# Half of the last stage's preparation moved into the scans before it, and the experts' units reordered and written out

## The reference, cut to what matters

```python
logits = xf @ gate_w
topk_vals, topk_idx = jax.lax.top_k(logits, 2)
gates = jax.nn.softmax(topk_vals, axis=-1)
h = jnp.einsum('nc,ech->neh', xf, w1) + b1[None]
h = jax.nn.gelu(h, approximate=False)
eo = jnp.einsum('neh,ehc->nec', h, w2) + b2[None]
comb = jnp.einsum('nk,nke->ne', gates, onehot)
out = jnp.einsum('ne,nec->nc', comb, eo)
```

## Time and profile before

| what | value |
|---|---|
| median of three runs | 977.3 us |
| the profiled execution, its own time | 978.52 us |
| its span | 976.7 us |
| busy in the span | TensorE 82%, VectorE 84%, ScalarE 68%, GpSimd 25% |
| first and last scan begin | 558.6 and 745.8 us |
| first expert product begins | 775.8 us |

### The profile page before, as it was taken

How to read it: one execution, slowest core, us unless ns; L and a number is a source line. 1 busy time by engine, 2 the same in 40 slices (tenths; PEclk the granted TensorE clock), 3 DMA queues, 4 the chain that set the end, 5 groups by cost and what they waited for, 6 DMA issues and landing times.

```text
span 976.7 us, 13030 instructions
## 1 busy us (share of the span) xinstructions
PE 801.6 (82%) x4241; PEld 414.7 (42%) x4241; DVE 818.1 (84%) x764; ACT 668.0 (68%) x1233; POOL 239.6 (25%) x132
## 2 busy tenths in 40 slices
PE   4579989999999999986375475677665679999998
PEld 2312212221222222223353355555554548888886
DVE  6788858887888888895888889999999846888886
ACT  2305757776777777775133597999994368888885
POOL 3800000000000000010100057888987501221220
PEclk9857979999999999999778688999999579999999
DMA  8422321212022110001200234455552021221221
GB/s 187 114 65 61 82 76 34 61 34 64 31 70 79 47 53 12 12 12 39 64 0 6 86 110 154 152 198 190 202 205 90 0 90 61 69 66 64 65 65 43
DMA packets 41524, 76.05 MB, mean 78 GB/s; under 512 B 7560, under 2 KB 25456, under 8 KB 40432
## 3 DMA queue, kind: packets, MB, share of 16 engines
q1 hardware_dynamic: 41464, 75.30, 24.7%
HBM read 64.99 MB, written 8.85 MB: 76 GB/s over the span
## 4 chain that ended last, share of the span: by engine, by line
PE 54%; ACT 17%; DVE 17%; issue 5%; SPq 4%; DMA 1%; POOL 0%; ACTq 0%; DVEq 0%; POOLq 0%
PE ps L1441 12%; PE ps L1462 11%; ACT dtb L912 8%; PE ps L1412 6%; PE ps L1696 6%; PE ps L1697 6%; PE ps L1698 6%; ACT abar L886 5%; DVE nmax L1066 3%; DVE hst L1201 2%; PE ps L1513 1%; SPq L521 1%; SPq L531 1%; DVE fx L454 1%; DVE fx L455 1%
## 5 line engine op out<-in xcount | busy, mean ns | idle before, releaser
L789 ACT ACTIVATE prob<-ps 128x512 f32<-128x512 f32 x512 | 265.0, 605 | 114.5 <-PE ps L1441 112.1
L1069 DVE TENSOR_REDUCE nmax_k<-ps 128x2 f32<-128x1024 f32 x224 | 262.4, 1219 | 45.5 <-PE ps L1412 44.3
L1441 PE MATMUL ps<-qs,ks 96*128 96x512 bf16 x512 | 165.8, 396 | 8.3 <-ACT prob L789 3.8
L717 POOL TENSOR_TENSOR hc<-hst,cbr 128x1024 f32<-128x1024 f32 x64 | 154.6, 2438 | 35.3 <-DVE hst L1201 23.7
L1201 DVE TENSOR_TENSOR_SCAN hst<-abar,ps 128x1024 f32<-128x1024 f32 x64 | 142.8, 2273 | 4.0 <-ACT abar L886 2.1
L1462 PE MATMUL ps<-prob,vq 128*16 128x512 f32 x1024 | 135.9, 608 | 0.8 <-ACT prob L789 0.7
L1284 DVE TENSOR_TENSOR act_l<-act_t,act_h 128x1024 fp32r<-128x1024 f32 x64 | 91.0, 1431 | 37.2 <-ACT act_h L996 37.2
L1441 PEld LDWEIGHTS ps<-qs,ks 96*128 96x128 bf16 x512 | 40.1, 98 | 169.5 <-ACT prob L789 109.0
L992 ACT ACTIVATE act_t<-ps,b_now 128x512 f32<-128x512 f32 x128 | 82.9, 683 | 25.4 <-PE ps L1698 25.4
L912 ACT ACTIVATE dtb<-dtxt,bt 128x128 f32<-128x128 f32 x328 | 99.8, 389 | 0.0
L1611 PE MATMUL ps<-ident,dtb 128*128 128x128 f32 x328 | 50.4, 291 | 51.2 <-DVE hst L1201 41.6
(11 more groups left out here) (192 smaller groups left out, 1146.6 us busy)
## 6 DMA issues: line engine op xcount, KB each, us to landing
cbr<-s_dram SPq DMA_DIRECT2D x64, 512.0 KB, 4.2
gate<-c_dram SPq DMA_DIRECT2D x8, 1024.0 KB, 7.5
qs<-q_dram SPq DMA_DIRECT2D x16, 288.0 KB
ks<-k_dram SPq DMA_DIRECT2D x48, 96.0 KB
o_dram<-o_sb SPq DMA_DIRECT2D x16, 256.0 KB, 2.0
wf<-in_L_ffn_w SPq DMA_DIRECT2D x8, 256.0 KB, 2.8
wfq<-in_L_ffn_w SPq DMA_DIRECT2D x8, 256.0 KB, 3.1
km<-k_dram SPq DMA_DIRECT2D x56, 32.0 KB
```

The costliest lines, as they stand in the source:

```text
L717: nc.gpsimd.tensor_tensor(hc[:, slot], hst[:, slot], cbr[:, slot], ALU.mult).then_inc(s_hc, 1)
L789: nc.scalar.activation(prob[:, n % 8], ps[:, 4 + (first + n) % 3], ACT.Exp, scale=ATT_SCALE).then_inc(s_exp, 1)
L1069: nc.vector.tensor_reduce(nmax_k[:, half, kk, 2 * pair:2 * pair + 2, qt], ps[:, 2 * pair:2 * pair + 2, :], AX.X, ALU.max, negate=True).the ...
L1441: nc.tensor.matmul(ps[:, 4 + (first + n) % 3], ks[p][:, kt // 4, j, kt % 4 * P:(kt % 4 + 1) * P], qs[p][:, half, j, :], start=True, stop=T ...
```

## The change

For batch 0, the norm, the turning and rounding, the logits, the choice of experts, the gates and the split of expert 0's weights now stand among the scans of batch 1, at written positions m. The ranking by 8 x 8 comparisons becomes two rounds of maximum, comparison and removal (`pick_two`). For batch 1, the same steps stand among the first units, which take experts 0 and 1 on batch 0's chunks first. The first product of unit 0 waits for the last scan, and the last two totals come behind it. b2 is added in the instruction that multiplies by the gate, and the matmuls and copies for it are gone, as are the copies of b1 (L1273). The remainder of x is taken from PSUM. Dynamic loops over scans and units are written out. Buffers of the last stage are laid over those of the scans with spacers (`over`), so that what is written early lies on nothing in use. The core of the diff:

```diff
-UNITS = 2 * CHUNKS
+UNITS = EXPERTS * CHUNKS
+FIRST_UNITS = ((0, 0), (0, 1), (1, 0), (1, 1), (0, 2), (0, 3), (1, 2), (1, 3))
+FAR_BELOW = -3.0e38
...
+        def unit_of(m):
+
+            return FIRST_UNITS[m] if m < len(FIRST_UNITS) else divmod(m, CHUNKS)
+
+        def last_unit(e):
+
+            return max(m for m in range(UNITS) if unit_of(m)[0] == e)
...
+            def first_gates(b):
+                w = slice(b * SEQ, (b + 1) * SEQ)
+                sp.wait_ge(s_combt, b + 1)
+                sp.dma_start(c_dram[:, w], comb_t[:, w]).then_inc(s_comb_out, 16)
+                sp.wait_ge(s_comb_out, 16 * (b + 1))
+                for e in range(2):
+                    sp.dma_start(gate[:, e, w], c_dram[e:e + 1, w].to_broadcast([P, SEQ])).then_inc(s_gate[e], 16)
+
+            def next_expert(e):
+                sp.wait_ge(s_w_l, e - 1)
+                load_expert(e, e % 2)
+
+            first_gates(0)
+            next_expert(2)
+            next_expert(3)
+            first_gates(1)
+            for e in range(2, EXPERTS):
+                sp.wait_ge(s_moe, 2 + last_unit(e - 2) + 1)
+                load_gate(e, e % 2)
+                if e + 2 < EXPERTS:
+                    next_expert(e + 2)
...
+            def upper_weights(e):
+
+                p = e % 2
+                pool.wait_ge(s_w12[p], 32 * (e // 2 + 1))
+                if e >= 2:
+                    pool.wait_ge(s_l2, 2 + last_unit(e - 2) + 1)
                 nc.gpsimd.tensor_tensor(w12_h[:, p], w12[p], zero[:].unsqueeze(2).to_broadcast([P, 2, HIDDEN]),
                                         ALU.subtract).then_inc(s_w_h, 1)
+
+            def lower_weights(e):
+
+                p = e % 2
                 pool.wait_ge(s_w_h, e + 1)
                 nc.gpsimd.tensor_tensor(w12_l[:, p], w12[p], w12_h[:, p].bitcast(F32), ALU.subtract).then_inc(s_w_l, 1)
 
...
+            pool.wait_ge(s_normed, 6)
+            for m in range(BATCH * NSTATE):
+                outflow(m)
+                if m == 14:
+                    upper_weights(0)
+                if m == 22:
+                    lower_weights(0)
+                if m == 41:
+                    norm_pool(3, 0)
+            upper_weights(1)
+            lower_weights(1)
             norm_pool(3, 1)
+            for e in range(2, EXPERTS):
+                upper_weights(e)
+                lower_weights(e)
...
+            def second_gate(b):
+                act.wait_ge(s_diff, b + 1)
+                nc.scalar.activation(top[:, 3, 8 * b:8 * b + 8], top[:, 2, 8 * b:8 * b + 8], ACT.Exp).then_inc(s_ediff, 1)
+
+            def turned_gates(b):
+                act.wait_ge(s_combt_ps, b + 1)
+                nc.scalar.activation(comb_t[:, b * SEQ:(b + 1) * SEQ].rearrange("e (g t) -> e g t", t=BANK), ps[0:EXPERTS, 4:6],
+                                     ACT.Copy).then_inc(s_combt, 1)
...
+                if m == 41:
+                    norm_act(3, 0)
+                if m == 51:
+                    turn_and_round(0)
+                    turn_and_round(1)
+                if m == 59:
+                    second_gate(0)
+            turned_gates(0)
...
+            for m in range(UNITS):
+                unit(m)
+                if m == 1:
+                    norm_act(3, 1)
+                if m == 2:
+                    turn_and_round(2)
+                    turn_and_round(3)
+                if m == 4:
+                    second_gate(1)
+                if m == 5:
+                    turned_gates(1)
...
+            def lower_x(c):
+                w = slice(c * BANK, (c + 1) * BANK)
+                dve.wait_ge(s_xh, c + 1)
+                nc.vector.tensor_tensor(xl[:, w], ps[:, 4 + c % 2], xh[:, w].bitcast(F32), ALU.subtract).then_inc(s_xl, 1)
+
+            def pick_two(b):
+
+                t = slice(8 * b, 8 * b + 8)
+                row = lambda n: bc(top[:, n, t], EXPERTS)
+                order = first[:].unsqueeze(1).to_broadcast([P, 8, EXPERTS])
+                dve.wait_ge(s_lgps, b + 1)
+                dve_step(nc.vector.tensor_copy(lg[:, t], ps[:, 4, 0:8 * EXPERTS].rearrange("p (t e) -> p t e", e=EXPERTS)))
+                left = lg[:, t]
+                for n in range(2):
+                    dve_step(nc.vector.tensor_reduce(top[:, n, t], left, AX.X, ALU.max))
+                    dve_step(nc.vector.tensor_tensor(key[:, n, t], left, row(n), ALU.is_equal))
+                    dve_step(nc.vector.tensor_tensor(key[:, n, t], key[:, n, t], order, ALU.mult))
+                    dve_step(nc.vector.tensor_reduce(top[:, 6 + n, t], key[:, n, t], AX.X, ALU.max))
+                    dve_step(nc.vector.tensor_tensor(is01[:, n, t], key[:, n, t], row(6 + n), ALU.is_equal))
+                    if n == 0:
+                        dve_step(nc.vector.scalar_tensor_tensor(comb[:, t], is01[:, 0, t], FAR_BELOW, lg[:, t], ALU.mult, ALU.add))
+                        left = comb[:, t]
+                nc.vector.tensor_tensor(top[:, 2, t], top[:, 1, t], top[:, 0, t], ALU.subtract).then_inc(s_diff, 1)
+
+            def gates(b):
+
+                t = slice(8 * b, 8 * b + 8)
+                dve.wait_ge(s_ediff, b + 1)
+                dve_step(nc.vector.tensor_scalar(top[:, 4, t], top[:, 3, t], 1.0, None, ALU.add))
+                dve_step(nc.vector.reciprocal(top[:, 4, t], top[:, 4, t]))
+                dve_step(nc.vector.tensor_tensor(top[:, 5, t], top[:, 3, t], top[:, 4, t], ALU.mult))
+                for n in range(2):
+                    ins = nc.vector.tensor_tensor(is01[:, n, t], is01[:, n, t], bc(top[:, 4 + n, t], EXPERTS), ALU.mult)
+                dve_step(ins)
+                nc.vector.tensor_tensor(comb[:, t], is01[:, 0, t], is01[:, 1, t], ALU.add).then_inc(s_comb, 1)
...
+                if m == 20:
+                    dve_step(nc.vector.tensor_reduce(first[:], tri[:], AX.X, ALU.add))
+                    dve_step(nc.vector.tensor_scalar(first[:], first[:], -1.0, float(EXPERTS), ALU.mult, ALU.add))
                 if m == NSTATE + 2:
                     add_scanned(0)
...
+                if m == 36:
+                    norm_dve_a(3, 0)
+                if m == 40:
+                    norm_dve_var(3, 0)
+                if m == 44:
+                    norm_dve_scale(3, 0)
+                if m == 49:
+                    lower_x(0)
+                    lower_x(1)
+                if m == 53:
+                    pick_two(0)
+                if m == 56:
+                    gates(0)
...
+            def combine(m):
+
+                e, c = unit_of(m)
                 w = slice(c * BANK, (c + 1) * BANK)
-                if c == 0:
-                    dve.wait_ge(s_gate[e], 16 * (k + 1))
+                dve.wait_ge(s_gate[e % 2], 16 * (1 + c // 2 if e < 2 else e // 2 + 2))
                 dve.wait_ge(s_l2, m + 3)
                 dve.wait_ge(s_moe, m + 2)
-                nc.vector.tensor_tensor(term[:], ps[:, 6 + u % 2], gate[:, e, w], ALU.mult).then_inc(s_term, 1)
-                dve.wait_ge(s_term, m + 1)
+                shift = b1t[:, EXPERTS * HT + e:EXPERTS * HT + e + 1]
+                if e == 0:
+                    nc.vector.scalar_tensor_tensor(acc[:, w], ps[:, 6 + m % 2], shift, gate[:, 0, w], ALU.add, ALU.mult).then_inc(s_moe, 1)
+                    return
+                nc.vector.scalar_tensor_tensor(term[:], ps[:, 6 + m % 2], shift, gate[:, e % 2, w], ALU.add, ALU.mult).then_inc(s_term, 1)
+                dve.wait_ge(s_term, sum(unit_of(j)[0] > 0 for j in range(m + 1)))
                 nc.vector.tensor_tensor(acc[:, w], acc[:, w], term[:], ALU.add).then_inc(s_moe, 1)
...
+            add_scanned(1)
+            second_parts(0)
+            norm_dve_a(3, 1)
+            second_parts(1)
+            norm_dve_var(3, 1)
+            combine(0)
+            norm_dve_scale(3, 1)
+            second_parts(2)
+            combine(1)
+            lower_x(2)
+            lower_x(3)
+            second_parts(3)
+            combine(2)
+            pick_two(1)
+            second_parts(4)
+            gates(1)
+            combine(3)
+            for m in range(5, UNITS):
+                second_parts(m)
+                combine(m - 1)
+                if m >= UNITS - 2:
+                    add_experts(m - UNITS + 2)
+            combine(UNITS - 1)
...
-            LAG = RING
+            LAG = RING + 1
...
+            def logits(b):
+                pe.wait_ge(s_xt, 12 + 2 * b + 2)
+                pe.wait_ge(s_xl, 2 * b + 2)
+                for t in range(8 * b, 8 * b + 8):
+                    mm = nc.tensor.matmul(ps[:, 4, t % 8 * EXPERTS:(t % 8 + 1) * EXPERTS], xt[:, t * P:(t + 1) * P], wgate[:],
+                                          start=True, stop=True)
+                mm.then_inc(s_lgps, 1)
+
+            def turn_gates(b):
+                pe.wait_ge(s_comb, b + 1)
+                for t in range(8):
+                    mm = nc.tensor.transpose(ps[0:EXPERTS, 4 + t // 4, (t % 4) * P:(t % 4 + 1) * P], comb[:, 8 * b + t, :], ident[:])
```

(35 more changed lines are left out.)

298 lines of the change are left out of this document (58 added, 240 removed).

## The result

Eight executions of the changed kernel have a median of 966.98 us (962.51 to 972.68); eight of the kernel before, on the same chip, 977.36 (975.67 to 978.48). The ratio is 0.9895, its 95% interval 0.9868 to 0.9921. Here the medians lie 10.4 apart; on the chip of e12_again, the same kernel once more, it is 8.6 (966.82 and 975.41). The single executions lie 10 us apart where those of before lie 3 apart, so single profiles are compared by stages, not by their totals. The profiled execution took 968.08 us, with a span of 965.7.

What follows compares the result with a forecast made beforehand. VectorE was taken to pace the scans and TensorE the units; 29.0 us gained behind the scans less 20.5 lost in them, 8.5 net, brought 977.3 to 968.8 us. Its own range was 964 to 974; 958 to 978 held 8 in 10.

Steps and rivals of the forecast that it cites:

- comes first behind its scan, 1.2 us: In the scans: norm_dve_scale starts ahead of the outflow, so it isn't held up and costs 1.2 us.
- the wait to 2.5: In the scans: an outflow holds up the first later VectorE step needing it until about 2.5 us behind its scan, once.
- ScalarE at nothing: In the scans: ScalarE's additions, 4.7 us against VectorE's 20.5, cost nothing, as it gets ahead by up to four scans.
- T: The end of the last scan, 748.1 us in the kernel before; the span was forecast to end at T + 199.6.
- the wait for unit 6: Behind the scans: remainders of unit 6, behind combine(4) and expert 2's weight split, make second product 6 start 3.4 us late.
- the rival of the clock: At the units' start: waits let the clock fall, two products cost 2.7 us more each, 974.2 us; chance 0.15.
- step 5: Behind the scans: the other 24 units take 130.8 us, to T + 190.1.
- The tail: From the end of second product 30 to the last addition: 9.4 us with the reordered turn_back, 6.25 before.
- the walk's 10: In the 60 us behind the last scan: TensorE idle for 10 us; above 15 us would show the prediction wrong.
- the stalls' absence: In the scans: small operations slip in beside outflows, T moves by 13.2 us instead of 20.5, 961.5 us; chance 0.17.
- a backlog of GpSimd over all six places: In the scans: each of six places waits 2.34 us longer, T moves by 34.5 us, 982.8 us; chance 0.10.
- the third rival: In the scans and behind them: extra waits eat the net gain, 977 us; chance 0.07.

Runs made afterwards that it cites:

- e12_again: The changed kernel once more, unchanged: 966.82 us, against 975.41 us for the kernel before on the same chip.
- e4_infl: The changed kernel with batch 0's norm_dve_scale, pick_two and gates behind the next input multiplication instead of right behind the scan: 963.54 us.
- e10_exp: The changed kernel with ScalarE's small exponential for batch 0 ahead of the factors of scan 58 instead of behind those of scan 59: scans 208.6 us.
- e5_pair: The changed kernel with two small reductions and a 64-column tensor_tensor, read by nothing, added on VectorE after six scans: scans 222.1 us.
- e1_behind: The changed kernel with all of batch 0's preparation back behind the last scan, unit order and b2 kept: 969.72 us, ratio 0.9944 to the kernel before.
- e7_gates: The changed kernel with gates(0), their turn and their copy moved out of the scans to behind the last scan: 962.95 us.
- e3_swap: The changed kernel with VectorE's remainders of unit 6 ahead of combine(4), the combination that waits for batch 1's gates: 963.3 us.
- e11_best: The changed kernel with e2_tail, e3_swap, e7_gates and e8_lag4 together, plus the scaling and pick_two moves of e4_infl: 954.26 us, ratio 0.9777 to the kernel before.
- e2_tail: The changed kernel with turn_back in its old order, behind second products 29 and 30: 966.61 us.
- e6_single: The changed kernel with three small reductions, read by nothing, added on VectorE after six scans: scans 213.9 us.
- e9_order: The changed kernel with the first eight units in plain order, all of expert 0, then expert 1: 978.08 us, ratio 1.003 to the kernel before.
- e8_lag4: The changed kernel with TensorE's totals four scans behind the fills instead of five: 964.13 us.

## Why the prediction was right, point by point

**The scans** were to pay 20.5 us and paid 21.3, of which 20.6 behind scan 20, where the insertions begin. In e12_again they paid 19.0, so that the sum came so close is in part luck. The mechanism was the one described: a step waits until the outflow under way ends. The terms, forecast and measured:

```
first             2.7   0.4   at the seam of two outflows
add_scanned(0)    1.5   1.4
norm_dve_a        3.9   3.7   (2.6 in e12_again)
norm_dve_var      1.2   1.1
norm_dve_scale    1.2   2.3   mis-sized
two lower_x       1.3   1.2
pick_two          5.2   5.1
gates             3.5   4.9   mis-sized
wait of an inflow 0     0.3
```

Two terms were too small and one too large, and they cancel. The step that failed for `norm_dve_scale` was "comes first behind its scan, 1.2 us". L391 took 2.34 us, held by the outflow of the scan before, which ended at 703.53; GpSimd was late by its own step of the norm (L415, 1.64 us at 697.25). e4_infl moved L391 by an input multiplication and got 1.25. For `gates` it was "the wait to 2.5" as the only hold-up: two outflows ran back to back there, and each held a step. For `first` it was that the outflow comes ahead of the tensor_scalar: this step began at 631.83, while one outflow was ending (631.95) and 0.07 us before the next began (631.90), and took 0.17 us. So 2.5 us behind the scan holds only where GpSimd is on time and comes first; what a place pays hangs on when GpSimd is released, by the outflow before, by its own steps or by TensorE's totals.

**ScalarE at nothing** was true in its effect and not in its reason. VectorE did wait 1.4 us for the exponential, since ScalarE's lead was gone (after `pick_two` it waits 3.5 us for the ring). It cost nothing, as e10_exp shows, for the hold-up ended at the same time.

**Behind the scans** 199.6 us were forecast and 199.1 measured. The first steps hold closely: the wait before turning x 1.9 us (forecast 2.6), the gates at T + 45.8 (48.4), the wait for unit 6 3.0 (3.4). Then the rival of the clock came in, in part. The prediction gave it 2.7 us a product; second product 6 ran at half speed throughout and second product 7 ended at T + 61.2, where step 5 started from 59.3. That this doesn't show is an error of step 5, which let second product 30 end at T + 187.4. From unit 7 to unit 30 are 23 x 5.45 = 125.4 us, so by its own numbers it should have been T + 184.7. Measured was T + 186.9. The slip of 2.7 us and the missing half-clock product are nearly equal: that this stage was hit within 0.5 us is luck. In e12_again it took 197.8 us. The tail was right: 9.6 us (9.4). TensorE's idle time in the 60 us behind the last scan was 60 - 54.5 = 5.5 us, less than the walk's 10.

**The range and the rivals.** Neither the stalls' absence (e5_pair) nor a backlog of GpSimd over all six places came true; something of it did at two, `norm_dve_scale` (1.1 us) and `gates`. The books of moving into the scans nearly balance by themselves (e1_behind), as the third rival had it for the whole change.

## What to carry to other kernels

Before work is moved under a saturated engine, price both ends. Here the preparation cost 20 us in the scans and saved about the same behind them, and the gain hung on letting TensorE start on the half that was ready with enough units to cover the other half (11 us lost without it). What leaving out b2's products added to it was not measured by itself. Inside such a stage put what may be held up where its engine has slack, even if it is held up longer there (e7_gates), and place the rest behind a step that the neighbour's instruction doesn't block (e4_infl). In an in-order queue, never let a step with a late transfer stand ahead of one that the next engine needs (e3_swap); what such repairs are worth adds up (e11_best, 12.6 us beyond the change).

## What the runs showed of the hardware that was not expected

- Where GpSimd's instructions follow one another, VectorE gets in a step between them and is held up again by the next: three groups of small steps in a row for 2.17, 2.01 and 2.26 us (e7_gates). GpSimd didn't let VectorE finish its short ones first.
- The clock does not fall alike after like waits. After the wait of 2.01 us in the tail it fell to half in the profile of e3_swap from the fifth matmul on (0.63 us each) and not in that of the changed kernel (0.39 each), whose instructions in the tail are the same. Of the eleven profiles with this wait (all but the kernel before, e2_tail and e11_best) it fell in five: e3_swap, e4_infl, e6_single, e7_gates and e9_order, at 1.1 to 1.6 us each. That is a part of the 10 us between executions. What makes the difference wasn't found. The Trainium skill (TensorE: Matmul & The Clock Gate, Part 1) says of a kernel's start that the number of slow matmuls differs between runs of one kernel. The traces show the like in the middle and at the end of one.
- One wait lends its time to the next: GpSimd, held up or waiting for a total at half clock, starts its outflow late, and which of VectorE's steps meets it differs between executions of one program (L374: 1.33 us or 0.17). In all twelve profiles that have L374 at this place the clock of TensorE in the 4 us before goes with it. It was 1.00 in six (the changed kernel, e2_tail, e5_pair, e7_gates, e8_lag4, e11_best): the outflow ran when L374 came, which took 1.33 or 1.34 us. It was 0.58 to 0.61 in the other six: the total was late, the outflow waited 2.7 us for it and began only behind L374, which took 0.17. So there the slower TensorE spared VectorE 1.2 us.
